# Unit 15 of an attention stage: denominators on TensorE without sums, a third probability buffer, and two norm tiles on GpSimd

## The reference

```python
x = x + attn_a(layernorm(x))
x = x + ffn(layernorm(x))
# attention: 16 heads of 32; keys and values are shared by the two query sets
scores = einsum('bhqd,bhkd->bhqk', q, k2) * scale      # q = q1 heads, then q2 heads
scores = where(causal, scores, min)
p = softmax(scores, axis=-1)
y = einsum('bhqk,bhkd->bhqd', p, v2)
y = y1 - sigmoid(x @ Wlam) * y2
x = x + y @ Wo
x = x + ffn(layernorm(x))
# ffn: gu = x @ ternary(w_gate_up); h = silu(gate) * up; rms_norm(h) @ ternary(w_proj)
```

## Time and profile before

| | us |
|---|---|
| median of 3 runs | 2064.17 (2063.1 to 2064.34) |
| the profiled execution, its own time | 2059.48 |
| its span, first to last instruction | 2056.6 |
| TensorE busy | 1972.4 (96%) |
| VectorE busy | 1331.6 (65%) |
| GpSimd busy | 882.9 (43%) |
| ScalarE busy | 828.2 (40%) |
| units 0 to 15 | about 835 to 1690 us of the span |

### The profile page before, as it was taken

How to read it: one execution, slowest core, us unless ns; L and a number is a source line. 1 busy time by engine, 2 the same in 40 slices (tenths; PEclk the granted TensorE clock), 3 DMA queues, 4 the chain that set the end, 5 groups by cost and what they waited for, 6 DMA issues and landing times.

```text
span 2056.6 us, 36719 instructions
## 1 busy us (share of the span) xinstructions
PE 1972.4 (96%) x15063; PEld 832.1 (40%) x15104; DVE 1331.6 (65%) x2622; ACT 828.2 (40%) x1259; POOL 882.9 (43%) x459
## 2 busy tenths in 40 slices
PE   7898999899999998999999999999999879899999
PEld 3444444444444443333333333333333334344444
DVE  5868686847847545566666666666667755775644
ACT  4534343425444411444434433344434442543431
POOL 3757575700000000566666667777776670000000
PEclk9999999999999999999999999999999999999999
DMA  8101011130000021000101010010000201000001
GB/s 240 35 27 36 31 37 31 29 125 1 1 0 1 0 57 20 22 17 22 22 22 22 12 26 13 22 22 22 2 22 7 93 2 41 1 0 21 21 1 41
DMA packets 71591, 60.19 MB, mean 29 GB/s; under 512 B 37312, under 2 KB 55744, under 8 KB 71168
## 3 DMA queue, kind: packets, MB, share of 16 engines
q1 hardware_dynamic: 64512, 45.27, 7.8%
q10 hardware_dynamic: 6912, 12.59, 1.9%
HBM read 43.02 MB, written 10.62 MB: 26 GB/s over the span
## 4 chain that ended last, share of the span: by engine, by line
PE 52%; DVE 5%; POOL 2%; ACT 1%; issue 1%; SPq 1%; DMA 0%; DVEq 0%; POOLq 0%; ACTq 0%
PE psum L128 9%; PE psum L1313 8%; PE psum L1219 8%; PE psum L1370 6%; PE psum L1353 6%; PE psum L152 5%; PE psum L1259 3%; PE psum L1349 2%; POOL b_totals L1599 2%; PE psum L1326 2%; PE psum L1270 1%; PE psum L1340 1%; DVE psum L1666 1%; DVE b_maxima L1671 1%; DVE b_down L1729 0%
## 5 line engine op out<-in xcount | busy, mean ns | idle before, releaser
L1599 POOL TENSOR_TENSOR b_totals<-b_totals,b_probs 128x2048 f32<-128x2048 f32 (+5 forms) x160 | 506.4, 3165 | 255.1 <-ACT b_probs L1515 249.0
L1666 DVE CUSTOM_DVE_ANT_0 psum<-psum,b_rest 128x384 f32<-128x384 f32 (+3 forms) x512 | 236.4, 524 | 200.1 <-PE psum L1313 199.7
L1515 ACT ACTIVATE b_probs<-psum 128x1024 f32<-128x1024 f32 (+3 forms) x320 | 228.8, 766 | 237.0 <-PE psum L1353 219.9
L447 PE MATMUL psum<-hT,a_win 128*128 128x512 f32 x640 | 292.2, 600 | 2.6 <-DVE a_parts L751 1.2
L128 PE MATMUL psum<-hT,b_early 128*128 128x512 f16 x1024 | 228.5, 382 | 9.8 <-DVE b_middle L214 6.9
L128 PE MATMUL psum<-hT,W 128*128 128x512 f16 x1024 | 224.6, 379 | 3.7 <-DVE a_win L214 3.6
L1671 DVE TENSOR_REDUCE b_maxima<-psum 128x2 f32<-128x1024 f32 x128 | 150.9, 1221 | 101.3 <-PE psum L1313 101.3
L447 PEld LDWEIGHTS psum<-hT,a_win 128*128 128x128 f32 x640 | 120.0, 192 | 130.3 <-issue 129.0
L128 PEld LDWEIGHTS psum<-hT,b_early 128*128 128x128 bf16 x1024 | 100.1, 98 | 135.5 <-issue 10.1
L1571 POOL MEMSET b_mask<- 128x128 f32 x1 | 0.2, 205 | 349.4 <-POOLq L279 349.4
L128 PEld LDWEIGHTS psum<-hT,W 128*128 128x128 bf16 x1024 | 100.0, 98 | 124.2 <-DVE a_win L214 6.5
(11 more groups left out here) (232 smaller groups left out, 3311.7 us busy)
## 6 DMA issues: line engine op xcount, KB each, us to landing
a_parts<-in_w_guT ACTq DMA_DIRECT2D x32, 256.0 KB, 2.7
ternary<-W SPq DMA_DIRECT2D x1, 6144.0 KB, 18.1
a_win<-in_w_inT SPq DMA_DIRECT2D x20, 256.0 KB, 7.6
a_parts<-in_w_pT ACTq DMA_DIRECT2D x16, 256.0 KB, 2.6
b_down<-lam_rows SPq DMA_DIRECT2D x32, 128.0 KB, 2.6
b_early<-ternary SPq DMA_DIRECT2D x8, 512.0 KB, 8.2
out<-x SPq DMA_DIRECT2D x16, 256.0 KB, 2.2
x<-in_x SPq DMA_DIRECT2D x3, 1024.0 KB, 8.0
```

The lines of the kernel that those rows point to most:

```text
L447: last = pe.matmul(ring(s, j), win[:, at:at + P], core["hT"][:, (i * KT + k) * BLK:(i * KT + k + 1) * BLK], start=(k == 0), stop=(k == KT ...
L1515: act.activation(held(u, s)[:, 2 * a:2 * a + 2, off:BLK], pair_banks(("score", u, s, a))[:, :, off:BLK], ACT.Exp, scale=SCALE).then_inc(ex ...
L1599: pool.tensor_tensor(acc, acc, held(u, s)[:, own, off:BLK], ALU.add).then_inc(summed, 1)
L1666: last = dve.tensor_tensor_reduce(scores, scores, row_mask[:, BLK - width:BLK], 1.0, -3e38, ALU.add, ALU.max, maxima[u % 2][:, at:at + 1])
```

## The change

- Unit 15 has no sums. TensorE multiplies each step's probabilities by ones as soon as they exist (`last_den`) and accumulates them in bank 7, just ahead of the weighing of the same step. `share_sum` goes, GpSimd adds nothing in unit 15, and `exps` waits for no sum of that unit.
- The denominators of unit 14, chunk 1, are made at step 1 of unit 15 (before: step 2); the copy of unit 15's chunk 0 stands at step 4 (before: 5).
- `EPILOGUE` on TensorE is now `last_den` of step 11, ahead of the last weighing; ScalarE's copy and VectorE's reciprocals of it stand ahead of the feed-forward part.
- A third probability buffer, for all units. It lies in `rest`, which grows from 3 to 5 tiles of 512 columns.
- `early_rows` lie in `lent` instead of in two buffers of their own; the last two tiles of `rest` take their place where `late_rows` and `tail_row` used them.
- Norm tiles 2 and 3 are made by GpSimd in unit 14, behind the sum of step 3.

```diff
@@ job_from
     r, w = divmod(u, 2)
+    if u == UNITS - 1:
+        return {(1, 1): ("den", u - 1, 1), (4, 0): ("den", u, 0)}.get((i, place))
@@ phase_rest
-        ..., rest = ..., sb("rest", 3 * BLK)
+        ..., rest = ..., sb("rest", (1 + HPT) * BLK)
-        prob = [probs[:, i * HPT * BLK:(i + 1) * HPT * BLK] for i in range(2)]
+        prob = [probs[:, i * HPT * BLK:(i + 1) * HPT * BLK] for i in range(2)] + [rest[:, BLK:(1 + HPT) * BLK]]
-        early_rows = [sb(f"early_rows{i}", D) for i in range(2)]
+        early_rows = [lent[:, i * D:(i + 1) * D] for i in range(2)]
@@ TensorE
+            def last_den(s):
+
+                c, kt = STEPS[s]
+                n, off = NTH["den", UNITS - 1, c], step_width(s)
+                if kt == 0:
+                    free(n)
+                for j in range(HPT):
+                    pe.wait_ge(exped, ((UNITS - 1) * NS + s) * 2 + j // 2 + 1)
+                    last = pe.matmul(bank[JOB_BANK[n]][HEAD_AT[j] * HD:(HEAD_AT[j] + 1) * HD, off:BLK],
+                                     core["ones"][:, 0:HD], held(UNITS - 1, s)[:, j, off:BLK],
+                                     start=kt == 0, stop=s == CHUNK_LAST[c])
+                if s == CHUNK_LAST[c]:
+                    last.then_inc(filled, 1)
...
                     scores(u, i)
+                    if u == UNITS - 1:
+                        if i == 2:
+                            last_den(0)
+                        if i >= 2:
+                            last_den(i - 1)
+                        weigh(*divmod(u * NS + i - 1, NS))
+                        if i == 1:
+                            fill(*PART_AT[u, 1, 1])
+                        if out_in(u, i):
+                            output(*out_in(u, i))
+                        continue
...
+            last_den(NS - 1)
             weigh(UNITS - 1, NS - 1)
...
-                    if i == 0 and m == 0:
-                        for job in EPILOGUE:
-                            fill_all(job)
@@ ScalarE, exps
-                elif summed_by(u, s) > 2:
-                    act.wait_ge(summed, summed_by(u, s) - 2)
-                    if summed_by(u, s) - 2 > EARLIER_SUMS:
-                        act.wait_ge(shared, summed_by(u, s) - 2 - EARLIER_SUMS)
-                    act.wait_ge(weighed, g - 1)
+                elif summed_by(u, s) > len(prob):
+                    read = summed_by(u, s) - len(prob)
+                    act.wait_ge(summed, min(read, ALL_SUMS))
+                    act.wait_ge(weighed, g - len(prob) + 1)
@@ GpSimd
+            def early_turn(blk, t):
+                n = blk * TPB + t
+                pool.wait_ge(turn_ready, n)
+                pool.wait_ge(filled, NTH[("norm", *divmod(n - 2, TPB))] + 1)
+                pool.tensor_scalar(early_rows[t % 2][:, :], x[:, n * D:(n + 1) * D], e_mv[:, 2 * n:2 * n + 1],
+                                   e_inv[:, n:n + 1], ALU.subtract, ALU.mult).then_inc(turn_ready, 1)
...
-                    if STEPS[s][1]:
+                    if STEPS[s][1] and u < UNITS - 1:
                         add_up(u, s)
+                    if u == UNITS - 2 and s == CHUNK_LAST[0]:
+                        early_turn(0, 2)
+                        early_turn(0, 3)
@@ VectorE
-                    if u == UNITS - 2 and (i + 1, 0) in NORM_AT:
+                    if u == UNITS - 2 and NORM_AT.get((i + 1, 0), 2) < 2:
                         early_turn(0, NORM_AT[i + 1, 0])
...
-                    if u == UNITS - 1 and STEPS[i][1]:
-                        share_sum(u, i)
...
+            for part in range(2):
+                invert(UNITS - 1, 1, part)
             ff.hidden_units(dve, 0, between=between(0))
```

More of the change, by code:

```diff
@@ L1002, in summed_by @@
     return sum(1 for t in range(NS) if STEPS[t][1]) * u + sum(1 for t in range(s + 1) if STEPS[t][1])
-EARLIER_SUMS = summed_by(UNITS - 2, NS - 1)
+ALL_SUMS = summed_by(UNITS - 2, NS - 1)
 def first_weights(sp, core, wq1, wq2, wk):
@@ L1029, in phase_rest @@
         early, middle, down = sb("early", 8 * S), sb("middle", 8 * S), sb("down", 4 * S)
-        totals, probs, rest = sb("totals", 2 * HPT * BLK), sb("probs", 2 * HPT * BLK), sb("rest", 3 * BLK)
+        totals, probs, rest = sb("totals", 2 * HPT * BLK), sb("probs", 2 * HPT * BLK), sb("rest", (1 + HPT) * BLK)
         kT_made, kT_turned = ([early[:, i * S:(i + 1) * S], middle[:, i * S:(i + 1) * S]] for i in range(2))
@@ L1071, in phase_rest @@
         out_done, out_added = sem("out_done"), sem("out_added")
-        shared = sem("shared")
         keys_turned = sem("keys_turned")
@@ L1090, in phase_rest @@
         bank, x, hT = core["banks"], core["x"], core["hT"]
-        late_rows = [y_part[0], y_part[1], early_rows[0], early_rows[1]]
+        last_rows = [rest[:, (3 + i) * BLK:(4 + i) * BLK] for i in range(2)]
+        late_rows = [y_part[0], y_part[1], last_rows[0], last_rows[1]]
         h16 = core["hT16"]
@@ L1098, in tail_row @@
         def tail_row(t):
-            return (early_rows[0], early_rows[1], wo_sl[0], last_bias)[t][:, :]
+            return (last_rows[0], last_rows[1], wo_sl[0], last_bias)[t][:, :]
         def turn_bank(t):
@@ L1124, in held @@
                 return heads(total[(u * CQ + c) % 2])
-            return heads(prob[(summed_by(u, s) - 1) % 2])
+            return heads(prob[(summed_by(u, s) - 1) % len(prob)])
         @block.sync
@@ L1265, in fill @@
                     pe.wait_ge(summed, summed_by(u, CHUNK_LAST[c]))
-                    if u == UNITS - 1:
-                        pe.wait_ge(shared, summed_by(u, CHUNK_LAST[c]) - EARLIER_SUMS)
                     for j in range(HPT):
@@ L1536, in _ @@
             weigh_out(UNITS - 1, 1)
+            for job in EPILOGUE:
+                copy_out(job)
             def between(i):
                 def hook(m):
-                    if i == 0 and m == 0:
-                        for job in EPILOGUE:
-                            copy_out(job)
                     if i == 0 and m == 14:
@@ L1596, in add_up @@
                     pool.wait_ge(summed, n - 1)
-                own = slice(0, 2 if u == UNITS - 1 else HPT)
-                acc = heads(total[(u * CQ + c) % 2])[:, own, off:BLK]
-                pool.tensor_tensor(acc, acc, held(u, s)[:, own, off:BLK], ALU.add).then_inc(summed, 1)
+                acc = heads(total[(u * CQ + c) % 2])[:, :, off:BLK]
+                pool.tensor_tensor(acc, acc, held(u, s)[:, :, off:BLK], ALU.add).then_inc(summed, 1)
             def take(u, c):
@@ L1673, in row @@
                         pair_banks(("row", u, n, a))[:, :, 0:width], AX.X, ALU.max).then_inc(row_max, 1)
[L1675 to L1684, removed]
             def negate(u):
@@ L1762, in early_turn @@
                     v.settle()
-                if n >= 2:
-                    dve.wait_ge(filled, NTH[("norm", *divmod(n - 2, TPB))] + 1)
                 dve.tensor_scalar(early_rows[t % 2][:, :], x[:, n * D:(n + 1) * D], e_mv[:, 2 * n:2 * n + 1],
@@ L1849, in hook @@
                 def hook(m):
-                    if i == 0 and m == 0:
-                        for part in range(2):
-                            invert(UNITS - 1, 1, part)
                     if i == 0 and 4 <= m < 4 + QT:
```

## The result

| | before | after |
|---|---|---|
| median, first measurement | 2063.64 us (4 runs) | 2051.85 us (4 runs) |
| ratio, 95% interval | | 0.9942 (0.9926 to 0.9958) |
| second measurement | 2063.22 us (21 runs) | 2053.68 us (5 runs) |
| ratio, 95% interval | | 0.9951 (0.9938 to 0.9965) |
| profiled execution, own time / span | 2059.48 / 2056.6 us | 2050.75 / 2048.9 us |

The change makes the kernel faster by 11.8 us in the first measurement and 9.5 us in the second. The direction and the three places of the gain were right, the size was too small.

A forecast was written before the change was run, and what follows sets the result against it. TensorE bounds the middle units; units 14 and 15 lose time to pauses behind GpSimd sums and a late norm tile. Gains 2.8 + 1.5 + 2.2 = 6.5 us give 2057.7 for the median, range 2053.5 to 2061.5.

The forecast's parts named there:

- the three places of the gain: Unit 14 gains 2.8 us, unit 15 1.5 and the start of the feed-forward part 2.2.
- the cap: Unit 14: GpSimd's pauses before unit 15's bias total 2.89 us, so unit 15 can start 2.8 us earlier, no more.
- the price of a tile: Unit 14, norm tiles on GpSimd: 1.3 us each taken, 4.10 the upper bound; no cost up to 3.8 each.
- At 0.97 that is 8.7 us: Unit 15, TensorE's path: nine full groups of new denominators at 0.97 us each add 8.7 us.
- my lower bound of 0.89: Unit 15: 0.89 us a denominator group, the distance between weighing groups, would give 0.7 us more gain.
- The hand-over of bank 7: Unit 15, step 4: first chunk 1 denominators wait until ScalarE empties bank 7; a new wait of 0.3 us.
- I carry the gain over to the median: Whole run: the 6.5 us gain, summed against the profiled 2059.48 us, is applied to the median, 2064.17.
- 1 (the gain of unit 14 does not come): Unit 14: tiles outlast GpSimd's gap or its full queue grows; 2060.5 with the whole gain lost; chance 0.14.
- 2 (unit 15 as long as before): Unit 15: TensorE waits for exponentials instead, or bank 7 costs 1.9 us or more; 2059.2 to 2060.4; chance 0.14.
- 3 (groups one after the other): Unit 15, TensorE's path: new groups do not run side by side, 34 us slower, 2092; chance 0.04.
- 5 (nothing measurable): Counted pauses come back elsewhere, as in the feed-forward part's waits for VectorE; 2062; chance 0.06.
- 4 (more than forecast): Unit 15: denominators and weighing join without a gap, 0.89 a group, and small pauses go too; 2055.9; chance 0.14.

The follow-up runs named there:

- The reordering: Changed kernel with unit 15's bias spread first, plus step 4's denominators put behind its weighing; unit 15 33.2 us against 33.7, ratio to the kernel before 0.9929.
- tile 2 earlier: Kernel before, all on VectorE, with norm tile 2 moved from the head of step 5 to the end of step 3 in unit 14; ratio 0.9987.

## Why the prediction was right or wrong

**The middle units and the third buffer: right.** A unit in the middle takes 55.3 us as before, and two buffers in place of three change nothing.

**Unit 14: the mechanism and the cap right, the price of a tile low.** Forecast 2.8 us; against the same profile 2.65. The tile collided with a sum (0.45 against 4.10 us), GpSimd's pauses went, and the bias at the end of its queue set the start of unit 15; moving it one place ahead gave the 2.5 us that the cap had kept. A tile took 2.07 us on GpSimd and not 1.3, 0.8 us more a tile than I had put in, and the two started at 1614 and 1617; it cost nothing, since it was in cover all the same: 2.26 us of the gap stayed free, not 3.2. As for the 6 us of a first call, of which the GPSIMD Engine Reference of the Trainium skill warns (2.1), this trace has none, though these two tiles are the first operations of their kind on GpSimd: GpSimd stood idle for 0.34 and 0.99 us ahead of them, each starts 0.2 us after the end of the transpose that it waits for (1613.26 + 0.66 and 1616.33 + 0.66), and what follows is in time.

**Unit 15: the mechanism right, its sum 1.9 us too long.** Forecast 35.5 us at full clock; measured 33.6 to 33.7 in four traces (34.3 where the new pause brought the low clock, 0.95). The failed step is the price of the new groups, "At 0.97 that is 8.7 us". I read 0.97 from one distance, 1666.37 to 1667.34. Measured by addition a group costs 0.86 us, 1.0 us less for nine; that was below even my lower bound of 0.89. The other 0.9 us lie in waits that the sum left in as work. The row of a pause shows less than the pause costs. Before:

```profile
1674.30 0.29 PE L1340 MATMUL psum<-b_later_key,b_ident_b 128*32 128x128 bf16 x8
...
1676.70 0.35 PE L1349 MATMUL psum<-b_last_bias,b_ones_b 32*128 32x384 bf16 x4
```

The eight products ahead of the first pause take 0.29 us to their end, the eight behind it 0.23 (from 1676.47 in the earlier trace rows to 1676.70): 0.52 us, where the sixteen in one piece take 0.34 in the changed kernel (1675.42 to 1675.76). That is 0.18 us at each of three pauses, and 0.2 in the same way ahead of the fourth. The scores of step 7, which went out in two pieces (at 1669.53 and 1669.80), took 0.24 longer than those of a step in one piece. Together these are 1.0 us that went with the pauses. The hand-over of bank 7 made a pause of 0.65 us where 0.16 stood before, and the scores of step 5 wait 0.2 less ahead of it: 0.3 in all, as forecast. The reordering gave 0.5 back.

**Start of the feed-forward part: right.** 2.2 forecast, 16.05 - 13.83 = 2.2 measured against the same profile; no wait of TensorE at its third group.

**From the profile to the median: wrong.** The failed step is "I carry the gain over to the median". It takes for granted that the profiled execution is as typical of the kernel before as of the kernel after. It was not: against two other traces of the kernel before, it gained 3.8 and 4.0 us ahead of unit 14, where the change does nothing and every kernel varies (1596.5 to 1601.5 us in 14 traces), and 1.5 us in unit 14 behind the pause of 3.03 us, where the change does act. Against these two traces the change brings 4.1 us in unit 14 (without the 0.75 us ahead of the pause), 3.4 in unit 15 (2.7 with low clock) and 2.2 to 3.6 at the start of the feed-forward part, 9.0 to 11.1 in all. Over all traces in which a stretch has the form of the kernel before or of the changed one, the means differ by 3.5, 3.2 and 2.6 us, 9.3 together (unit 14 again without the 0.75 us where they stand; unit 15 of "tile 2 earlier" is left out, as its low clock follows a pause that the kernel before does not have). With the 0.8 us outside the span, of which the last paragraph of this section tells, that is 10.1. The measurements say 9.5 and 11.8.

So what the forecast lacked lies in three places of much the same size: against these two traces 1.3 us in unit 14, 1.2 to 1.9 in unit 15 and 0 to 1.4 at the start of the feed-forward part. The distance of the two spans, 2056.6 - 2048.9 = 7.7 us, is near the parts against the same profile (2.65 + 2.7 + 2.2) by luck: unit 14 began 1.6 us later in the trace after, and what follows the first tail output took 348.8 us in place of 350.6. That rest is 348.8 to 350.6 us in traces of both kernels (348.8 in one of the kernel before, 350.5 in another of the changed one), so no part of it is the change's.

**The rivals.** 1 (the gain of unit 14 does not come), 2 (unit 15 as long as before), 3 (groups one after the other) and 5 (nothing measurable) fell: 53.9 us, 33.6 us, 0.86 us a group, 9.5 us or more. 4 (more than forecast) came: both of its causes in unit 15 were there, the cheaper groups and the small waits, 1.9 us for the 1.8 that it had been given, but it knew nothing of the low clock.

One thing is left open. The own time of an execution is longer than its span by 1.8 to 2.9 us, 2.6 in the median, in 36 executions of the kernel before, and by 1.8 in all nine of the changed kernel. The variants whose unit 15 is the new one have 1.8 to 2.0, those with the old one 1.8 to 3.0. That is 0.8 us of the gain. No trace shows where it lies. Nor does any run show why one execution has more low clock than another behind the same pause.

## What to carry to other kernels

A pause of TensorE has two prices: its length, and the low clock that may follow, which varies from one execution to the next. So a gain read from one profile should be set against the spread of the runs and their granted clocks before it is carried to the median, and removing long pauses is worth more than a profile with little low clock shows. A pause in an engine's timeline can also cost more than its row says: compare the steps from start to start. Where products of the critical engine replace another engine's late work, move only what is late: keeping five of the ten sums beside TensorE's own work was 3.0 us better than moving all ten. When a stall goes, read what stands at the head of the next queue; here one line's order on GpSimd was worth 2.5 us.

## What the runs showed of the hardware

- A VectorE operation on float32 in SBUF (tensor_scalar, 128x512) took 0.45 us with GpSimd idle and up to 4.10 us over a running GpSimd sum of 4.51, ending 0.3 us after it. The same operation took 2.07 us on GpSimd, more than GpSimd's add of two tensors of that size (1.28 us).
- A group of four products on 32 columns (128x512, float32) added 0.86 us to a full TensorE queue, measured by four more of them.
- Four pauses of TensorE, 9.0 us by their rows, cost 0.75 us more than that: sixteen products took 0.52 us around a pause and 0.34 in one piece.
- Behind the same pause of 3.06 us unit 15 ran at a granted clock of 0.95 in one execution and 1.00 in another, 34.29 against 33.58 us. The window of the first stands in the section on the result; the second:

```profile
1654.97:1688.55 33.58, 32.06 (x464) 12.92 (x465) 6.78 (x8) 20.09 (x28) 7.27 (x6) 1.00 0.01 1
```
